# A four-layer conditioned transformer on one core: all places of the written-out order set anew, idle matmuls removed, and the router's condition term computed once at set-up

## What is computed

```
layer 0: x += gate * attn(adaLN(x), rope, block mask)       attention 0, 128 keys
         x += gate * attn(adaLN(x), context, key mask)      attention 1,  77 keys
         x += gate * (gelu(adaLN(x) W1 + b1) W2 + b2)        MLP m0
layer 1: x += attn(adaLN(x), adaLN(context)) Wp + bp         attention 2,  77 keys
layer 2: x += gate * attn(adaLN(x))                          attention 3, 128 keys
         x += attn(LN(x), context)                           attention 4,  77 keys
         x += gate * MLP(adaLN(x))                           MLP m1
layer 3: nx = LN(x); evidence = softmax(nx Wq (ctx Wk)^T) (ctx Wv)
         c = [nx, evidence, cond]                            cond: one row a sample
         probs = softmax(c @ router_W + router_b)            3 experts
         x += sigmoid(silu(c Wg1) Wg2) * (sum_e probs_e * (silu(c We1_e) We2_e) Wo)
```

## Time and profile before

| | |
|---|---|
| median of 3 runs | 773.54 us (773.48 to 774.25) |
| the profiled execution | 773.1 us, of which the span of its instructions 770.7 us |
| TensorE busy | 639.2 us (83% of the span), 6772 matmuls |
| DVE, ACT, POOL busy | 434.0 us (56%), 407.2 us (53%), 221.4 us (29%) |
| first turn (L1098), last turn | 36.1 us and 652.8 us after the span's start |
| chain that ended last | PE 56%, ACT 23%, DVE 15%, issue 4% |

### The profile page before, as it was taken

How to read it: one execution, slowest core, us unless ns; L and a number is a source line. 1 busy time by engine, 2 the same in 40 slices (tenths; PEclk the granted TensorE clock), 3 DMA queues, 4 the chain that set the end, 5 groups by cost and what they waited for, 6 DMA issues and landing times.

```text
span 770.7 us, 16690 instructions
## 1 busy us (share of the span) xinstructions
PE 639.2 (83%) x6772; PEld 370.0 (48%) x6772; DVE 434.0 (56%) x1147; ACT 407.2 (53%) x702; POOL 221.4 (29%) x320
## 2 busy tenths in 40 slices
PE   3869877988779887887788879877989888988897
PEld 1624433444434444444345445445546545476475
DVE  5386766646765667556655766475555666051332
ACT  3033634475357365736575456463676464835742
POOL 4131534223342334314431434151321241010000
PEclk9699988998889999999999899998899999998999
DMA  6520000000000000000000000000000000000000
GB/s 227 212 58 2 16 14 2 14 2 28 15 1 3 14 15 16 1 15 15 15 2 2 14 15 3 1 15 16 1 2 1 15 2 2 1 15 1 0 1 27
DMA packets 15602, 15.82 MB, mean 21 GB/s; under 512 B 1990, under 2 KB 13396, under 8 KB 15144
## 3 DMA queue, kind: packets, MB, share of 16 engines
q1 hardware_dynamic: 14952, 10.77, 4.6%
q10 hardware_dynamic: 576, 4.00, 1.3%
HBM read 13.67 MB, written 1.09 MB: 19 GB/s over the span
## 4 chain that ended last, share of the span: by engine, by line
PE 56%; ACT 23%; DVE 15%; issue 4%; POOL 2%; DMA 1%; DVEq 0%; SPq 0%; ACTq 0%; POOLq 0%
ACT P L603 13%; PE lin L1023 9%; PE lin L1039 9%; PE avp L1143 7%; PE big L1113 7%; DVE mhl L823 4%; PE big L1023 3%; PE big L1092 3%; PE big L1039 3%; PE big L1120 2%; PE lin L1049 2%; ACT xn L569 2%; DVE bst L770 2%; ACT hT L582 2%; ACT L603 2%
## 5 line engine op out<-in xcount | busy, mean ns | idle before, releaser
L823 DVE TENSOR_REDUCE mhl<-big 128x8 bf16<-128x616 f32 (+1 forms) x160 | 151.4, 963 | 99.7 <-PE big L1092 97.3
L536 POOL TENSOR_TENSOR qm<-qT,hm 128x512 f32<-128x512 f32 x80 | 87.3, 1091 | 129.6 <-ACT qT L562 75.8
L603 ACT ACTIVATE P<-big 128x1024 f32<-128x1024 f32 x64 | 62.0, 1020 | 89.0 <-PE big L1120 88.7
L603 ACT ACTIVATE P<-big,padcol 128x1024 f32<-128x1024 f32 x64 | 67.8, 1111 | 65.9 <-PE big L1120 65.8
L1113 PE MATMUL big<-qm,kT 32*128 32x512 f32 x640 | 95.0, 664 | 0.0
L499 POOL TENSOR_SCALAR rstd<-mv 128x4 f32<-128x4 f32 (+1 forms) x36 | 8.4, 233 | 298.8 <-DVE mv L776 298.6
L1023 PE MATMUL lin<-hT,W 128*128 128x512 f32 x150 | 87.2, 669 | 8.5 <-ACT hT L582 4.0
L1143 PE MATMUL avp<-P,Vp 128*32 128x128 f32 x2560 | 94.0, 292 | 0.0
L522 POOL TENSOR_TENSOR kbm<-kT,hm 128x308 bf16<-128x308 f32 (+1 forms) x80 | 69.1, 864 | 58.5 <-PE big L1092 43.0
L1143 PEld LDWEIGHTS avp<-P,Vp 128*32 128x32 f32 x2560 | 70.1, 116 | 28.6 <-issue 24.5
L1092 PE MATMUL big<-kbm,qb 32*128 32x308 bf16 (+1 forms) x320 | 52.9, 341 | 33.4 <-ACT P L603 30.3
(11 more groups left out here) (207 smaller groups left out, 981.7 us busy)
## 6 DMA issues: line engine op xcount, KB each, us to landing
gring<-gate_rows SPq DMA_DIRECT2D x20, 256.0 KB, 3.3
W<-in_w ACTq DMA_DIRECT2D x2, 1152.0 KB, 13.2
hid<-in_ws SPq DMA_DIRECT2D x2, 768.0 KB, 5.9
W<-in_w ACTq DMA_DIRECT2D x1, 1088.0 KB, 8.3
x<-in_x SPq DMA_DIRECT2D x4, 256.0 KB, 11.0
out<-x SPq DMA_DIRECT2D x4, 256.0 KB, 2.0
ctx<-in_ctx SPq DMA_DIRECT2D x4, 154.0 KB
ctxT<-in_ctxT SPq DMA_DIRECT2D x4, 154.0 KB
```

What stands on the lines that cost most here:

```text
L536: nc.gpsimd.tensor_tensor(qm[:, j % 2], q.broadcast_to([128, 4, T]), mask.broadcast_to([128, 4, T]), ALU.mult).then_inc(qm_ready, 1)
L603: nc.scalar.activation(P[:, 8 * half:8 * half + 8, :], big[:, 2 * half:2 * half + 2, :].rearrange("p g (h q) -> p (g h) q", h=4), ACT.Exp, ...
L823: v.tensor_reduce(mhl[:].rearrange("p (g c) -> p g c", c=32)[:, 2 * half:2 * half + 2, 0:4], big[:, 2 * half:2 * half + 2, 0:4 * kw].rearr ...
```

## The change

The slot table is new as a whole; the `v` projections of attentions 1 to 4 become chains of their own; the idle matmuls are gone; the router's condition term is computed once at set-up (`anclog`) and added where `rb` was.

TensorE units by position in the job, slots below `END` (counted from the two tables; `stat` and `apply` not counted):

| slot | 4j | 4j+1 | 4j+2 | 4j+3 |
|---|---|---|---|---|
| before | 62 | 43 | 55 | 39 |
| after | 111 | 15 | 41 | 31 |

The units placed from `END` on are 103 before and 104 after. Jobs with no TensorE unit in slot 4j and three idle matmuls: 38 before; no idle matmul after. The core of the diff:

```diff
-T_ANCHOR, T_COND, NT = 18, 25, 26
+T_ANCHOR, NT = 18, 25
@@ CHAINS
-    [("p1", "k"), ("l4", "stat"), ("o0", "y"), ("l4", "apply"), ("l1", "stat"), ("l4", "t"), ("p1", "v"),
-     ("l1", "apply"), ("l1", "t"), ("p1", "q")],
+    [("p1", "k"), ("l4", "stat"), ("o0", "y"), ("l4", "apply"), ("l1", "stat"), ("l4", "t"), ("l1", "apply"),
+     ("l1", "t"), ("p1", "q")],
...
+    [("p1", "v")],
+    [("p2", "v")],
+    [("p3", "v")],
+    [("p4", "v")],
@@ SLOTS (two of its rows)
-    (1, 2): [62, 62, 64, 70, 75, 75, 94, 95, 99, 106],
-    (2, 2): [132, 132, 135, 138, 143, 144, 146, 147, 149, 149, 150, 151, 156, 156, 160, 161, 164, 170],
+    (1, 2): [68, 71, 72, 78, 80, 80, 83, 88, 104],
+    (2, 2): [128, 130, 132, 136, 140, 142, 144, 146, 148, 148, 150, 150, 160, 161, 162, 165, 170],
...
-IDLE = [j for j in range(JOBS) if not any(slot == 4 * j and u[1] not in ("stat", "apply") for slot, u, s in PLACED)]
@@ build
-        NCOND, NCONST, NREST, NFIRST = 2, 15, 3, 2
+        NCOND, NCONST, NREST, NFIRST = 2, 13, 3, 2
-                             (ind48[:], ind_in), (row, row_in), (vcol, vcol_in), (gbrow, gb_in),
-                             (onesp[:], onesp_in), (rw[:], rw_in), (rb[:], rb_in[:, 0].partition_broadcast(128))):
+                             (row, row_in), (vcol, vcol_in), (gbrow, gb_in), (rw[:], rw_in), (rb[:], rb_in[:, 0].partition_broadcast(128))):
@@ DVE, set-up
+            v.memset(ones[:], 1.0)
+                v.tensor_tensor(condr[:], condT[:].unsqueeze(2).broadcast_to([128, B, 3]),
+                                rw[:, 2:3, :].broadcast_to([128, B, 3]), ALU.mult)
+                v.tensor_copy(tab[:, T_ANCHOR:T_ANCHOR + 7, :], modv[:, 14:21, :]).then_inc(
+                    lin_free[lin_bank("z0", 0, "mods")], 1)
-                v.tensor_copy(tab[:, T_ANCHOR:T_ANCHOR + 7, :], modv[:, 14:21, :]).then_inc(
-                    lin_free[lin_bank("z0", 0, "mods")], 1)
-                v.tensor_copy(tab[:, T_COND, :], condT[:]).then_inc(tab_done, 1)
+                i.then_inc(tab_done, 1)
+                v.tensor_tensor(anclog[:], avp[:, 256:256 + 3 * B].rearrange("p (b e) -> p b e", e=3),
+                                rb[:].unsqueeze(1).broadcast_to([128, B, 3]), ALU.add)
@@ DVE, lg
-                    v.tensor_tensor(pr3[s][:, 0], lt, rb[:].unsqueeze(1).broadcast_to([128, GB, 3]),
-                                    ALU.add).then_inc(lin_free[lin_bank(st, s, "lg")], 1)
+                    v.tensor_tensor(pr3[s][:, 0], lt, anclog[:, s * GB:(s + 1) * GB, :], ALU.add).then_inc(lin_free[lin_bank(st, s, "lg")], 1)
@@ TensorE, set-up
+                mm(avp[:, 256:256 + 3 * B], ones[:], condr[:].rearrange("p b e -> p (b e)"), start=True, stop=True)
@@ TensorE, lg and the list
-                        parts = [h[:, b * T:(b + 1) * T], ev[:, b * T:(b + 1) * T], anchor[:, b, :]]
+                        parts = [h[:, b * T:(b + 1) * T], ev[:, b * T:(b + 1) * T]]
-                            i = mm(lin_ap(st, s, "lg")[:, 3 * b:3 * b + 3], a, rw[:, c, :], start=(c == 0), stop=(c == 2))
+                            i = mm(lin_ap(st, s, "lg")[:, 3 * b:3 * b + 3], a, rw[:, c, :], start=(c == 0), stop=(c == 1))
-                        if u in IDLE:
-                            keep_warm(3)
```

More of the change, by code:

```diff
@@ L292, in build @@
         oneb = sb("oneb", [128, 512], BF16)
-        ind48 = sb("ind48", [128, H])
         hm4 = sb("hm4", [128, 4])
@@ L296, in build @@
         indb = sb("indb", [128, 4, 128], BF16)
-        onesp = sb("onesp", [128, 4, 32])
+        ones = sb("ones", [128, 128])
+        condr = sb("condr", [128, B, 3])
+        anclog = sb("anclog", [128, B, 3])
         mqk8 = sb("mqk8", [128, T], U8)
@@ L728, in tables @@
                         for r, nm in enumerate(("g2", "b2") if k == 6 else ("gam", "bet")):
-                            v.tensor_copy(tab[:, 2 * k + r, :], c_(nm).broadcast_to([128, B]))
+                            i = v.tensor_copy(tab[:, 2 * k + r, :], c_(nm).broadcast_to([128, B]))
                     elif k > 0:
@@ L1123, in scores_t @@
                             i.then_inc(st_full, 1)
-            def keep_warm(n):
-                for _ in range(n):
-                    mm(mtpf[:], identb[:], oneb[:], start=True, stop=True)
             def av(j):
@@ L1202, in mixture @@
                     lin_taken(pe, st, s, "ev")
-                    anchor = tab[:, T_COND, s * GB:(s + 1) * GB].unsqueeze(2).broadcast_to([128, GB, T])
                     take(st, s, "lg")
                     for b in range(GB):
-                        parts = [h[:, b * T:(b + 1) * T], ev[:, b * T:(b + 1) * T], anchor[:, b, :]]
+                        parts = [h[:, b * T:(b + 1) * T], ev[:, b * T:(b + 1) * T]]
                         for c, a in enumerate(parts):
-                            i = mm(lin_ap(st, s, "lg")[:, 3 * b:3 * b + 3], a, rw[:, c, :], start=(c == 0), stop=(c == 2))
+                            i = mm(lin_ap(st, s, "lg")[:, 3 * b:3 * b + 3], a, rw[:, c, :], start=(c == 0), stop=(c == 1))
                     give(st, s, "lg", i)
```

## The result

The changed kernel takes 652.4 us (median of 4 runs, 650.5 to 655.1) beside 773.9 us (773.5 to 777.8) of the kernel before: ratio 0.842 [0.838, 0.847], 121.5 us less. The forecast was 736 us with a range from 714; it had the direction, and a third of the size.

A forecast was written before the change was run, and what follows sets the result against it. TensorE's own work bounds most of the time, a cross-engine chain in each job the rest. Terms -17.6, -12.2, -3, -4, +3, +3, -7 sum to -38 us off 773.54, giving 736 us; range 714 to 766.

The forecast's parts named there:

- Check of the count: Jobs' stage: bare jobs of 5.0 or 6.0 us plus both slot sums give 545 us, 623 measured; other 78 kept.
- Slots 4j+2/3 and 4j/4j+1: Jobs: fewer exposed units in the last two slots gain 17.6 us; less excess over 1.6 us in the first two, 12.2.
- Idle matmuls (-3): 38 jobs: removing 114 idle matmuls mostly gives nothing, as exponentials hide them; gain 3 us, bounds 0 and 24.
- DVE (-4): Three blocks with `y` and `stat` in one slot 4j: `stat` moved later, 1.3 us each, 4 us gained.
- Tables (+3): ScalarE: 46 function changes against 40, seven more in the jobs at 0.4 us each; loss 3 us, bounds 0 and 9.
- Rival five: ScalarE: each table switch costs load plus an equal wait, 16 us in place of 3; 749 us, chance 0.07.
- Clock (+3, bounds -15 and +30): TensorE's clock in the jobs: less busy in light jobs, but long stalls rarer; a loss of 3 us taken.
- Router (-1.7): Condition's matmuls, 0.86 us a group: two groups in the tail give 1.7 us; two in crowded jobs already counted.
- Tail (-7, bounds 2 and 12): Behind the last job: new order covers 5 of 6.2 us of waits, plus 1.7 from the router; gain 7 us.
- the third: Jobs of 77 keys: without idle matmuls TensorE's clock falls more; 785 us, sign a mean clock under 0.90; chance 0.10.
- The second: Slot 4j: moved units' DVE and ScalarE readers delay maxima and exponentials, half of 30 us returns; 751 us, chance 0.19.
- The fourth: Jobs: new places also take a third off the unexplained 78 us of stalls; 712 us, chance 0.12.

The follow-up runs named there:

- the four parts: Changed kernel with old places of chains 0 and 1, chain 2, chains 3 and 4, or the rest with the tail: 698.5, 699.0, 698.9, 699.8 us.

## Why the prediction was wrong

**The failed step** is under "Check of the count": the 545 us of the count against 623 measured, and of the difference "the other 78 us are stalls of other engines, table loads and the clock. They are not explained by position, and I keep them but for the terms below." After, the count is 515 and the stage 518: the 78 us are 3. That is 75 us of the gain in one line of the sum, where I had 4 (DVE), 3 (idle matmuls) and a loss on the clock and on the tables. The step had no reason: that position does not explain a stall does not say that new places leave it.

*Slots 4j+2/3 and 4j/4j+1 (-17.6 and -12.2).* Their sum of 30 us is consistent with the runs, which never measured it alone: position acts through stalls and clock as well (+34 us for a count of +21 in the new list; +23 for -11 in the old one, with 45 idle matmuls fewer).

*Idle matmuls (-3).* This is wrong as a term by itself. Their removal from the old list costs 25 us, outside my bounds of 0 and 24 of gain, since I priced only their place on the queue and not what they did for the clock. In the new list real units fill all but 7 of the slots 4j, and three in each job cost 18.

*DVE (-4).* The mechanism is right, the size too small. One pair costs 1 us, near the 1.3 said. But 7 pairs went to 1, and other DVE work that stood ahead of the maxima, or of their turned copy, was moved too: the turns' waits go from 22.0 to 7.9 us and those of the transposed scores from 11.5 to 1.7, 24 us together.

*Tables (+3).* 47 loads stand in the trace as forecast, but the sign was wrong, for I counted loads and not where they stand. The chain that ended last (rows: start, us, engine and line; a load has no tile) had 20 of the 41 loads of before on it, 25.7 us, the one of the earlier trace rows among them; of the 47 after it has 9, 11.5 us. Before, then after:

```profile
601.35 1.28 ACT L603
```
```profile
414.05 1.28 ACT L631
...
416.63 1.28 ACT L622
```

So up to 14 us of the gain can be loads that left the chain; no run isolates them. Rival five's price of 2.6 us a switch is not seen: 45 of the 47 loads start 0.02 us behind the function before them, and 31 are followed by the next one at 0.01 us.

*Clock (+3, bounds -15 and +30).* It has the wrong sign and lies outside its bounds: lower-level time over the span went from 89 to 24 us; at the third of a microsecond measured above, that is about -22. The rows' price (2.7 us for 6.8) was near.

*Router (-1.7).* It is 1.8 in the tail, as said; the 4.6 between the medians is not clear of noise.

*Tail (-7, bounds 2 and 12).* The windows give -15.5: the order 8 to 12, the router 1.8, and the clock the rest or a part of the order (the tail is at 1.00 now, 0.94 in the earlier trace rows).

Of the rivals, the third's mechanism is real in the old list: without idle matmuls the clock is 0.893 there, under the 0.90 named as its sign, and the time goes up. In the new list, also without idle matmuls, the waits are fewer and the clock is 0.98. The second's is real too, by the turns' waits of the run with all units in slot 4j; the new places avoid it. The fourth, "the stalls go too", was right in kind and stopped at a third, for no reason that a row gave (and a third of 78 off 736 is 710, not 712). Its argument against, that the rotary work stays, did not hold as a limit.

As a sum, with the count's 30 us unmeasured: count 30, clock about 22, tail's order about 10, router 2 to 5. Some 55 us of the 121.5 are left, and I read them as stalls of single jobs, for DVE and ScalarE, that the new list does not have. The windows give the same size another way: in the jobs the waits fell by 52 us and the idle matmuls, which stood mostly in waits, by 31; less the count's 30, that is 53 us. The waits for the maxima and their turned copy are 24 of these, and the table loads may be up to 14 more, if the two do not overlap. The rest I cannot give to single units: taking back any one of the four parts costs 48 us. So the failed step is shown, and the size of the stalls as far as the count's 30 us hold; which pair of units makes each is open.

## What to carry to other kernels

When a static order over several engines is set anew as a whole, the difference between a count by position and the measured time is not a constant to carry over: it can be most of what the change wins. Bound it at both ends, at nothing and at all of it. Price an idle matmul by what the clock does around it, never only by its place in the queue: 114 in a list with waits were worth 25 us, and 240 in one with few cost 18. Count a table load by whether it stands on the chain, not by how many there are. And see what else a moved number changes: `IDLE` followed the slots, so a test of position was also one of idle matmuls.

## What the runs showed of the hardware

In a kernel that is 80% busy on TensorE, the old list without idle matmuls, the clock fell 26 times in the jobs with no wait over 3.3 us from the first turn on, and more of the span was at 1.2 GHz (171 of 801 us) than TensorE waited in all (157 us). A microsecond at the lower level costs about a third of one here. The same matmuls are busy for 40 us more over the 82 us more at that level, and the time grows by 25 to 30; that the difference lies under waits for other engines is my reading, and no run isolates it. An activation table load takes 1.28 us; the next function can start 0.01 us behind it. Six more of them came with a shorter time, with 9 on the chain that ended last instead of 20.
